# Transposing gathered rows as float32r instead of float32 in the first layer of a graph network kernel

## The reference

```
h = concat(x_[senders], x_[receivers])          # here senders = src, receivers = dst
h = tanh(h @ W0 + b0);  h = tanh(h @ W1 + b1);  h = h @ W2 + b2
h = h * (e_embed @ Wg)
x = layernorm(x + segment_mean(h, senders))
```

## Time and profile before

| | |
|---|---|
| median of 3 runs | 2393.83 us (2392.34 to 2397.3) |
| the profiled execution's own time | 2392.13 us |
| its span, first to last instruction | 2390.1 us |
| mean granted TensorE clock | 0.915 |
| PE busy | 2049.8 us (86%) |
| PEld busy | 1779.5 us (74%) |
| DVE busy | 1604.7 us (67%) |
| ACT busy | 1340.5 us (56%) |
| POOL busy | 1552.7 us (65%) |

### The profile page before, as it was taken

The page is one execution under the profiler, slowest core; times in us unless marked ns, Lnnn a source line. Parts: engine busy times, 40 slices in busy tenths (PEclk is TensorE's granted clock), DMA queues, the critical chain, the costliest instruction groups (busy, mean ns, idle before and its releaser), DMA issues.

```text
span 2390.1 us, 42126 instructions
## 1 busy us (share of the span) xinstructions
PE 2049.8 (86%) x13381; PEld 1779.5 (74%) x13381; DVE 1604.7 (67%) x4219; ACT 1340.5 (56%) x2726; POOL 1552.7 (65%) x1204
## 2 busy tenths in 40 slices
PE   6799999999999999999999999999455666666660
PEld 6688888888888888888888888888444555554550
DVE  5566666666666666666666666666558877777776
ACT  4377777777777777777777777777340000000002
POOL 0427777876766667667667667664228777777774
PEclk9899999999999999999999999999777767777775
DMA  7787877876766667767767667665655655555553
GB/s 279 225 210 174 199 158 158 170 152 147 157 146 150 155 144 152 155 141 156 154 140 157 153 140 156 154 139 110 175 125 127 145 142 145 142 141 138 147 129 117
DMA packets 235934, 370.78 MB, mean 155 GB/s; under 512 B 35746, under 2 KB 168693, under 8 KB 235707
## 3 DMA queue, kind: packets, MB, share of 16 engines
q0 software_dynamic: 101232, 188.20, 40.3%
q1 hardware_dynamic: 134475, 179.80, 25.7%
HBM read 270.43 MB, written 97.45 MB: 154 GB/s over the span
## 4 chain that ended last, share of the span: by engine, by line
PE 67%; POOL 19%; issue 6%; DMA 4%; DVE 2%; ACT 1%; SPq 0%; POOLq 0%; ACTq 0%; DVEq 0%
POOL Hg L1302 18%; PE bank L1371 16%; PE bank L1372 16%; PE bank L1373 16%; PE bank L1414 7%; PE bank L1423 4%; PE bank L1440 3%; PE bank L1474 2%; PE bank L1473 2%; DMA accA<-ystage,to_a 1%; POOL fin L1362 1%; DMA TB<-stB 1%; PE bank L1536 1%; DMA TA<-stA 1%; DMA HT<-hst 0%
## 5 line engine op out<-in xcount | busy, mean ns | idle before, releaser
L1267 POOL DMA_INDIRECT accA<-ystage,to_a x391 | 653.1, 1670 | 206.8 <-issue 115.6
L1273 POOL DMA_INDIRECT GA<-TA,src_c x391 | 438.5, 1122 | 407.6 <-ACT ystage L1644 183.7
L1302 POOL DMA_INDIRECT Hg<-HT,src_c x391 | 434.8, 1112 | 182.8 <-issue 118.8
L511 DVE TENSOR_TENSOR h2l<-h2f,h2h 108x512 fp32r<-108x512 f32 (+1 forms) x294 | 203.1, 691 | 219.7 <-ACT h2h L1644 219.7
L1373 PE MATMUL bank<-h1h,W1l 128*108 128x512 f32 (+1 forms) x882 | 347.5, 394 | 0.0
L1371 PE MATMUL bank<-h1h,W1h 128*108 128x512 f32 (+1 forms) x882 | 346.7, 393 | 1.0 <-DVE h1l L511 1.0
L1372 PE MATMUL bank<-h1l,W1h 128*108 128x512 f32 (+1 forms) x882 | 346.2, 393 | 0.0
L1371 PE MATMUL bank<-W2h,h2h 108*128 108x256 f32 x1173 | 332.0, 283 | 0.4 <-DVE mf L639 0.4
L1372 PE MATMUL bank<-W2l,h2h 108*128 108x256 f32 x1173 | 332.3, 283 | 0.0
L1373 PE MATMUL bank<-W2h,h2l 108*128 108x256 f32 x1173 | 329.1, 281 | 0.0
L1805 ACT ACTIVATE drop<-neg_m 128x1 f32<-128x1 f32 x98 | 28.9, 295 | 495.0 <-DVE neg_m L874 495.0
(11 more groups left out here) (190 smaller groups left out, 4668.4 us busy)
## 6 DMA issues: line engine op xcount, KB each, us to landing
TW<-TB SPq DMA_DIRECT2D x196, 203.0 KB, 3.3
ef<-in_eT SPq DMA_DIRECT2D x97, 256.0 KB, 4.2
bcast_i<-in_src_row SPq DMA_DIRECT2D x97, 256.0 KB, 4.7
HB<-hist SPq DMA_DIRECT2D x98, 130.0 KB, 2.6
rel<-RL SPq DMA_DIRECT2D x97, 128.0 KB, 4.9
rem<-RD SPq DMA_DIRECT2D x48, 256.0 KB, 4.7
TB<-stB SPq DMA_DIRECT2D x24, 406.0 KB, 3.3
accA<-zeros SPq DMA_DIRECT2D x4, 1677.0 KB, 12.9
```

What stands on the lines that cost most here:

```text
L511: return dve.tensor_tensor(o, full, hi.bitcast(f32), ALU.subtract)
L1267: return pool.indirect_dma_start(out=table, out_offset=bass.IndirectOffsetOnAxis(ap=rows, axis=0), in_=sums, in_offset=None, compute_op=AL ...
L1273: pool.indirect_dma_start(out=GA[0:n, b % (GAR * BLOCKS_PER_GROUP), :], out_offset=None, in_=TA, in_offset=bass.IndirectOffsetOnAxis(ap=sr ...
L1302: pool.indirect_dma_start(out=Hg[0:n, slot, :], out_offset=None, in_=HT, in_offset=bass.IndirectOffsetOnAxis(ap=src_c[0:n, b:b + 1], axis= ...
```

## The change

GA becomes a float32r tile (the indirect transfer writes it through a float32 view), a float32r copy of the identity is made, and the 1564 transposes of the edge pipeline take both operands and their output as float32r. Before the pipeline's loop PE transposes the first 128 by 128 part of the first gathered block once as float32r and once as float32, into two PSUM banks; DVE copies the one, compares it with the other, takes the maximum over a row and adds 1e30 times it to `eps`, so that any difference would spoil the output. The name "ones" moves to the last of these.

```diff
+        ident_r = sb("ident_r", [P, P], f32r)
...
+        differs = sb("differs", [P, P + 2])
...
-        GA = sb("GA", [P, GAR * BLOCKS_PER_GROUP, H0], f32, sa)
+        GA = sb("GA", [P, GAR * BLOCKS_PER_GROUP, H0], f32r, sa)
...
+        s_twice = sem("s_twice")
...
             const(dve.tensor_scalar(ident[:, :], iota_row[:, :], p_f[:, :], None, ALU.is_equal))
+            const(dve.tensor_copy(ident_r[:, :], ident[:, :]))
...
-            const(dve.memset(ml[:, :, :, OUT:AW].bitcast(f32), 0.0), "ones")
+            const(dve.memset(ml[:, :, :, OUT:AW].bitcast(f32), 0.0))
+
+            dve.wait_ge(s_twice, 1)
+            const(dve.tensor_copy(differs[:, 0:P], PY[0][:, 0:P]))
+            const(dve.tensor_tensor(differs[:, 0:P], differs[:, 0:P], PY[1][:, 0:P], ALU.not_equal))
+            const(dve.tensor_reduce(differs[:, P:P + 1], differs[:, 0:P], AX.X, ALU.max))
+            const(dve.scalar_tensor_tensor(eps[:, :], differs[:, P:P + 1], 1.0e30, eps[:, :], ALU.mult, ALU.add), "ones")
...
-                    out=GA[0:n, b % (GAR * BLOCKS_PER_GROUP), :], out_offset=None, in_=TA,
+                    out=GA[0:n, b % (GAR * BLOCKS_PER_GROUP), :].bitcast(f32), out_offset=None, in_=TA,
...
-                    pe.matmul(PT[u % 2][0:k1(c), j * P:j * P + n],
+                    pe.matmul(PT[u % 2][0:k1(c), j * P:j * P + n].bitcast(f32r),
                               GA[0:n, b % (GAR * BLOCKS_PER_GROUP), c * P:c * P + k1(c)],
-                              ident[0:n, 0:n], is_transpose=True, start=j == 0, stop=False)
+                              ident_r[0:n, 0:n], is_transpose=True, start=j == 0, stop=False)
...
+            pe.wait_ge(s_ga[0], group_arrivals(GAR, 0))
+            pe.matmul(PY[0][:, 0:P].bitcast(f32r), GA[:, 0, 0:P], ident_r[:, :], is_transpose=True, start=True, stop=True)
+            pe.matmul(PY[1][:, 0:P], GA[:, 0, 0:P].bitcast(f32), ident[:, :], is_transpose=True, start=True, stop=True)\
+                .then_inc(s_twice, 1)
```

## The result

The changed kernel takes 2352.84 us (median of 4 runs, 2351.07 to 2357.55), the kernel before 2393.09 us in the 4 runs beside it; the ratio is 0.984 with a 95% interval of 0.981 to 0.9865. The profiled execution took 2351.07 us with a span of 2349.0 us.

The account below looks back on a forecast made before the run. PE was taken to bound the pipeline. Cheaper transposes (-50.8 us), the pipeline's end (+0.8) and the test (+0.4) gave -49.6 us from 2392.1, or 2342.5; with 1.7 us for a median, 2344 us, range 2311 to 2397 us.

Parts of the forecast that it names:

- What bounds the kernel, and that PE stays last: Edge pipeline: PE never idles, the period is 16.36 us; the tightest slack of 0.81 us loses 0.2 to 0.4 us.
- Moving side: Pipeline transposes: streaming 128 identity columns falls from 110 ns to the float32r matmul's rate, 58 ns.
- Weight side of a transpose: Transposes with 128 columns of weights: price between 58 and 110 ns, taken as 84 ns; narrow ones are not load-bound.
- the short load: Weight load with a record of 141 ns, as float32 transposes have, forecast to repeat every 57 ns.
- the long one: Weight load with a record of 192 ns, as float32r matmuls have, repeating every 108 ns at best.
- The step from a record 51 ns shorter to a load of 57 ns: Transpose's load: record of 141 ns against 192 ns, so it was taken to repeat every 57 ns instead of 108.
- The sum over the loop: 1173 wide transposes save 30.5 us and 391 narrow ones 20.3 us, together 50.8 us.
- The test, the identity's copy, the gathers: Before and around the loop: the test's two PE transposes add 0.4 us; its DVE part, the copy and the gathers nothing.
- No change: Rival: TensorE handles four-byte transposes alike for both types, so the time stays at 2394 us; chance 0.29.
- a split into two instructions: Rival: each float32r transpose is issued as two instructions of 110 ns, +172 us, 2566 us; chance 0.06.
- The short load for all: Rival: all 1564 transposes cost 58 ns, saving 81.3 us, 2314 us; chance 0.22.
- The full binding of the long load: Rival: wide transposes at 108 ns save 2 ns each, the 391 narrow ones 52 ns, 2372 us; chance 0.12.

Follow-up runs that it names:

- e2: Only the 1173 transposes with 128 columns of weights made float32r, the narrow ones left float32, against the kernel before: ratio 0.991 (0.9875 to 0.994).
- e1: Only the 391 transposes of the 22-column chunk made float32r, the wide ones left float32, against the kernel before: ratio 0.990 (0.986 to 0.993).
- Both reordered kernels with float32r: Changed kernel with transposes and receiver matmuls alternating in twos: 2476.2 us; changed kernel without the test, two chunks' transposes first, then their receiver matmuls: 2471.5 us.
- The first run of prices: Changed kernel plus 470 matmuls of several kinds before its test, one execution: float32r transposes with 128 columns of weights cost 86 ns each.
- the second run: Changed kernel plus warm-up, float32 transposes, plain float32r matmuls, then 200 float32 and 300 float32r transposes: 64 ns (half moved columns), 112 ns, 86 ns (float32r).

## Why the prediction was right, and what was mis-sized

*What bounds the kernel, and that PE stays last.* Right: PE is busy for all of the mid-pipeline window, and h1s lost 0.28 us of slack in the mean where 0.2 to 0.4 were forecast.

*Moving side.* Right: about one cycle a column, 58 ns forecast; about 60 ns alone, and a narrow chunk of 0.47 us.

*Weight side of a transpose.* I took the middle between the short load and the long one, 84 ns, for want of a nearer row. It measured 86 to 87. The value was right by what amounts to luck: neither row that I weighed is the price. A float32r transpose's load has the record of a float32 one (141 ns) and a price between that one's (at most 64 ns) and the plain matmul's (112 ns). The step from a record 51 ns shorter to a load of 57 ns came near for the float32 transpose and failed for the float32r one, whose record is as short.

*The sum over the loop, 50.8 us, is the term that was mis-sized: it measured 41.1.* The step that failed is "1173 x (110 - 84)": it prices each wide transpose by its own kind of load. The one that counts is the next instruction's. Behind every fourth transpose stands a receiver matmul with the long load, which the earlier trace rows already showed with 192 ns of record and the earlier trace rows with 108 ns of price. That is 294 x (109 - 84) = 7.4 us; the other 879 at 87 instead of 84 ns are 2.6 us. 50.8 - 10.0 = 40.8 us. Taken apart, run e2 measured 22.1 us for the 30.5 of the wide transposes, and run e1 19.4 us for the 20.3 of the narrow ones. Both reordered kernels with float32r bear the mechanism out, one in each direction.

*The test, the identity's copy, the gathers.* 0.4 us, nothing and nothing were forecast; no cost shows, though the forecast left out ACT's wait for the test. The time can't tell 0.4 us from nothing.

That 2344 us came within 9 us of the measured time rests on that middle value, so it is in part luck as well.

*The rivals.* No change, and a split into two instructions, are out by the records and the pitch. The short load for all is out in the kernel (2314 us) and by itself. The full binding of the long load, 2372 us, is the other half of the truth: its 109 ns hold, but for one transpose in four. The Trainium skill's rule behind it ("TensorE: Matmul & The Clock Gate", on LDWEIGHTS: the columns divided by 1.2, 107 ns for 128) agrees with the plain float32r matmuls (112 ns by themselves, 109 ns between the receiver matmuls' loads) and not with transposes, at 86 ns in float32r and at most 64 ns in float32.

## What to carry to other kernels

Price a short matmul by the larger of its own moving time and the weight load of the instruction behind it; once the moving side is made faster, count the pairs of neighbours and not the instructions. Narrow weights gain in full, wide ones stop at the load, and the order can be chosen so that a long load stands behind a long stream. A period over many groups, which repeated within 0.017 us of 16 here, resolves what run times with nearly 1% of scatter do not.

## What the runs showed of the hardware

The length of a weight load's record doesn't give its price: 141 ns stands for 86 ns between float32r transposes and for at most 64 ns between float32 ones. The load of the float32r transpose grows with its columns, 68 ns at 96 and 86 at 128, which is about half a nanosecond a column, and at 64 it hides behind the moving side. In the block that the kernel transposes both ways, float32r and float32 gave the same values; otherwise `eps` would have grown by 1e30.

Transposes alone brought TensorE's clock up and held it. The first run of prices, by window:

```profile
92.00:96.00 4.00, 3.75 (x19) 3.77 (x20) 0.00 (x0) 0.00 (x0) 3.04 (x4) 0.54 0.65 173
96.00:110.00 14.00, 14.00 (x131) 14.00 (x130) 0.00 (x0) 0.00 (x0) 5.67 (x6) 1.00 0.42 113
110.30:126.40 16.10, 16.10 (x242) 15.98 (x240) 0.00 (x0) 0.00 (x0) 0.00 (x0) 1.00 0.00 1
126.60:139.00 12.40, 12.40 (x79) 12.28 (x78) 0.00 (x0) 0.00 (x0) 0.00 (x0) 0.50 0.01 1
```

PE waits 14.6 us for the first gather before it and then does nothing but transposes up to 131 us. The granted clock goes from its lower to its full level (1.2 to 2.4 GHz) among float32 ones and stays there over the float32r ones. In the second run it is at 1.00 from 131.6 to 176.6 us, 45 us of float32 and then float32r transposes (the windows above). So the suspicion that float32r transposes let it fall, formed after the first run, fell too; why the clock dropped to half at about 126.4 us there, with PE busy before and after, stays open. The second run has such a drop too, among the plain float32r matmuls at about 124.8 us, again with PE busy throughout:

```profile
126.00:132.00 6.00, 6.00 (x32) 6.00 (x32) 0.00 (x0) 0.00 (x0) 0.00 (x0) 0.53 0.00 0
```

The Trainium skill ("TensorE: Matmul & The Clock Gate", on the PE-mode transpose) says that the full clock does not engage for transposes; these traces show it at 1.00 over 45 us of nothing else, and the measurement decides.
